# One gathered column of every two chunks (layer 0) and of every three (layer 1) is fetched by SyncE, row by row

## The reference

```python
zs = ZU[:, src, :]
zd = ZU[:, dst, :]
logits = (zs * zd).sum(-1) / scale
...
msgs = x[src]
summed = jax.ops.segment_sum(msgs, dst, num_segments=num_nodes)
```

## Time and profile before

| | us |
|---|---|
| median of the runs | 4623.81 |
| the profiled execution's own time | 4618.69 |
| its span | 4616.9 |
| POOL busy | 3353.7 (73%) |
| DVE busy | 2277.8 (49%) |
| PE busy | 930.4 (20%) |
| ACT busy | 778.7 (17%) |

### The profile page before, as it was taken

The page is one execution under the profiler, slowest core; times in us unless marked ns, Lnnn a source line. Parts: engine busy times, 40 slices in busy tenths (PEclk is TensorE's granted clock), DMA queues, the critical chain, the costliest instruction groups (busy, mean ns, idle before and its releaser), DMA issues. The chain is left out here.

```text
span 4616.9 us, 27468 instructions
## 1 busy us (share of the span) xinstructions
PE 930.4 (20%) x3111; PEld 610.2 (13%) x3111; DVE 2277.8 (49%) x9483; ACT 778.7 (17%) x1408; POOL 3353.7 (73%) x3541
## 2 busy tenths in 40 slices
PE   7301101112111000000094211222222221112037
PEld 7201001001001000000042100111111110001025
DVE  2107665665665565566563443443344344334447
ACT  2001001001001000000043222222222222222225
POOL 6677777777777777777565777777777777777765
PEclk6556555555556555555586555555555555555569
DMA  9713333333333222222275666666665666666579
GB/s 350 303 37 120 120 93 94 120 93 94 120 104 96 84 88 77 79 88 88 74 248 192 219 215 236 231 209 215 236 231 206 234 229 207 235 236 213 197 244 316
DMA packets 329803, 793.61 MB, mean 172 GB/s; under 512 B 78246, under 2 KB 216843, under 8 KB 300228
## 3 DMA queue, kind: packets, MB, share of 16 engines
q1 hardware_dynamic: 149906, 378.14, 23.0%
q0 software_dynamic: 139488, 279.69, 20.4%
q10 hardware_dynamic: 40274, 134.62, 7.4%
HBM read 420.40 MB, written 371.83 MB: 172 GB/s over the span
## 5 line engine op out<-in xcount | busy, mean ns | idle before, releaser
L473 POOL DMA_INDIRECT sb_big<-x,sb_idx x1564 | 1481.3, 947 | 513.0 <-issue 476.4
L473 POOL DMA_INDIRECT sb_big<-zu_rows,sb_idx x1564 | 1479.4, 946 | 490.4 <-issue 476.1
L1300 DVE SCALAR_TENSOR_TENSOR ps_V<-ps_V,sb_keepc,sb_big 128x256 f32<-128x256 f32 x1518 | 747.8, 493 | 132.5 <-ACT sb_big L901 79.3
L901 ACT COPY sb_big<-ps_V 128x1024 f32<-128x1024 f32 (+1 forms) x414 | 399.7, 966 | 1309.6 <-DVE ps_V L1300 1306.4
L654 PE MATMUL ps_T<-sb_ident,sb_xg 128*128 128x128 f32 x392 | 114.2, 389 | 2445.3 <-DMA sb_xg<-x 1232.4
L1300 DVE SCALAR_TENSOR_TENSOR ps_V<-ps_E,sb_keepc,sb_big 128x256 f32<-128x256 f32 x46 | 22.7, 492 | 1041.8 <-DMA sb_big<-x,sb_idx 1002.2
L1067 DVE TENSOR_TENSOR sb_big<-ps_V,sb_big 128x2176 f32<-128x2176 f32 x46 | 111.5, 2424 | 591.9 <-DMA sb_big<-zu_rows,sb_idx 591.9
L654 PEld LDWEIGHTS ps_T<-sb_ident,sb_xg 128*128 128x128 f32 x392 | 71.6, 200 | 2502.9 <-issue 1738.1
L1061 DVE TENSOR_TENSOR_SCAN ps_V<-ps_V,sb_big 128x34 f32<-128x34 f32 x2944 | 356.9, 208 | 17.4 <-issue 17.4
L1110 DVE TENSOR_TENSOR_SCAN sb_big<-ps_E,sb_big 128x34 f32<-128x34 f32 x2944 | 355.3, 203 | 1.6
L473 POOL DMA_INDIRECT sb_hn<-rows,sb_nidx x196 | 191.4, 976 | 87.6 <-issue 54.9
(11 more groups left out here) (229 smaller groups left out, 1732.5 us busy)
## 6 DMA issues: line engine op xcount, KB each, us to landing
rows<-sb_big SPq DMA_DIRECT2D x46, 3072.0 KB, 10.6
rows<-sb_big SPq DMA_DIRECT2D x46, 1280.0 KB, 10.5
rows<-sb_big ACTq DMA_DIRECT2D x46, 1224.0 KB, 5.4
z_at_start<-sb_big ACTq DMA_DIRECT2D x46, 1088.0 KB, 8.5
sb_big<-z_at_start SPq DMA_DIRECT2D x46, 1088.0 KB
sb_xg<-in_x_dram SPq DMA_DIRECT2D x42, 768.0 KB
own<-sb_hn SPq DMA_DIRECT2D x28, 896.0 KB, 11.5
sb_big<-own SPq DMA_DIRECT2D x28, 896.0 KB
```

Source lines behind the costliest of these rows:

```text
L473: pool.indirect_dma_start(to, None, table, bass.IndirectOffsetOnAxis(ap=index.bitcast(U32), axis=0), **more).then_inc(done, 16)
L901: act.copy(slot1[s][:, cols, :], V0[:, first_word:first_word + width].rearrange("p (c f) -> p c f", f=D)).then_inc(col_copied, 1)
L1300: dve.scalar_tensor_tensor(out=sums_at(j), in0=before, scalar=keepc[:, j:j + 1], in1=slot1[s][:, j, :], op0=ALU.mult, op1=ALU.add).then_in ...
```

## The change

After the change POOL gathers one column fewer in the second chunk of pairs 1 to 22 of layer 0, and one fewer in slot 1 of triples 0 to 14 of layer 1. SyncE fetches these columns in its place.

VectorE multiplies the row numbers of these columns by the length of a row once (`row_bytes`). For a column SyncE issues one transfer that lays its 128 byte offsets side by side in partition 0 (`stage_rows`), waits for it, then loads 16 offsets at a time into registers and issues one transfer per row, from the table at the offset in the register to one partition (`fetch_rows`).

In layer 0 the rows go to a tile of their own, `zx`; ScalarE copies it to the last column of `zs[1]` (`zx_copied`), VectorE waits for that copy before the product, and SyncE waits for it before it fetches the next. `fetch_zx(i)` brings the column of pair i+1 and stands behind `bg_load(0, i)` and ahead of `load_zd(i+1)`. In layer 1 the rows go straight to the last column of `slot1[1]`; `fetch_row1(i+1)` stands behind the stores of triple i and ahead of `bg_store(1, i)` and `bg_load(1, i+1)`, and waits until slot 1 of triple i is stored. VectorE waits for `row_fetched[1]` before slot 1's last column.

```diff
@@ -75,6 +75,8 @@
     GC = 4
     NGC = -(-C // GC)
     LOOK = S1 * C
+    RB = 16
+    U8 = mybir.dt.uint8
     NZ = 4
     assert FP * FQ == NF and FQ * FW <= C * F and CA % GC == 0 and NGC % 2 == 1 and C % GC == 2 and NG * GB == NB and NG % 2 == 0 and NCH % 2 == 0 and NG < NCH // S1 and 0 < ELAST <= COLS and NF * FW == E
     assert E <= EP and D == 2 * P
@@ -191,6 +193,9 @@
         end_i = sb("end_i", [P, 1], I32)
         keep_all = sb("keep_all", [P, 1])
         idx = [sb(f"idx{s}", [P, C], I32) for s in range(S1)]
+        row_bytes = [sb(f"row_bytes{k}", [P, n], I32) for k, n in ((0, NCH // 2), (1, NCH // S1))]
+        stage = sb("stage", [1, 2, P], I32)
+        zx = sb("zx", [P, F])
         nidx = [sb(f"nidx{s}", [P, GB], I32) for s in range(2)]
         zcar0 = sb("zcar0", [P, F])
         scar = sb("scar", [P, F + H])
@@ -275,6 +280,8 @@
         idx1_ready = sems("idx1_ready", S1); r_gathered = [sems(f"r_gathered{k}_", S1) for k in range(2)]
         keepc_made = sem("keepc_made"); col_summed = sem("col_summed"); col_copied = sem("col_copied")
         r_stored = sems("r_stored", S1); car1_saved = sem("car1_saved")
+        rows_scaled = sem("rows_scaled"); stage_loaded = sems("stage_loaded", 2); row_fetched = sems("row_fetched", 2)
+        zx_copied = sem("zx_copied")
         DA = 15
         NW = 5
 
@@ -283,6 +290,9 @@
         gate = sem("gate")
 
         block = ctx.enter_context(nc.Block())
+
+        def zs_landed(i, s):
+            return 16 * (C + (C - s) * i)
 
         def edge_cols(dram, c):
 
@@ -368,24 +378,55 @@
             sp.wait_ge(z_scattered, 16 * NB)
             sp.wait_ge(zcar_loaded, 16)
 
+            rows_at = [sp.alloc_register(f"row{k}") for k in range(RB)]
+
+            def stage_rows(layer, i):
+                with nc.allow_non_contiguous_dma(reason="a word of each partition"):
+                    sp.dma_start(stage[0:1, layer, :], row_bytes[layer][:, bass.ds(i, 1)]
+                                 ).then_inc(stage_loaded[layer], 16)
+
+            def fetch_rows(layer, to, table, width):
+                flat = table.rearrange("(a n) f -> a (n f)", a=1).bitcast(U8)
+                for p0 in range(0, P, RB):
+                    sp.load(rows_at, stage[0:1, layer, p0:p0 + RB])
+                    for k in range(RB):
+                        at_byte = sp.snap(rows_at[k], min_val=0, max_val=(N - 1) * 4 * width)
+                        sp.dma_start(to[p0 + k:p0 + k + 1, :].bitcast(U8), flat[:, bass.ds(at_byte, 4 * width)]
+                                     ).then_inc(row_fetched[layer], 16)
+
             def load_zd(i):
                 for s in range(2):
                     wait(sp, zd_used[s], i)
                     sp.dma_start(zd[s], edge_cols(z_at_start[0:EP, :], 2 * i + s)).then_inc(zd_loaded[s], 16)
 
+            def fetch_zx(i):
+                stage_rows(0, i + 1)
+                sp.wait_ge(stage_loaded[0], 16 * (i + 1))
+                sp.sem_inc(gate, 1)
+                wait(sp, zx_copied, i)
+                sp.sem_inc(gate, 1)
+                fetch_rows(0, zx[:, :], zu_rows, F)
+
             load_zd(0)
             bg_load(0, 0)
+            sp.wait_ge(rows_scaled, 2)
+            fetch_zx(0)
             with sp.Fori(1, NG - 1) as i:
                 load_zd(i)
                 bg_store(0, i - 1)
                 bg_load(0, i)
+                fetch_zx(i)
             load_zd(NG - 1)
             bg_store(0, NG - 2)
             bg_load(0, NG - 1, rows=TAIL)
+            fetch_zx(NG - 1)
             load_zd(NG)
             bg_store(0, NG - 1)
-            with sp.Fori(NG + 1, NCH // 2) as i:
+            fetch_zx(NG)
+            with sp.Fori(NG + 1, NCH // 2 - 1) as i:
                 load_zd(i)
+                fetch_zx(i)
+            load_zd(NCH // 2 - 1)
 
 
             def node_in(layer, i, s, rows=P):
@@ -415,6 +456,14 @@
                 sp.wait_ge(n_stored[0][s], 32 * (NG // 2))
 
 
+            def fetch_row1(i):
+                stage_rows(1, i)
+                sp.wait_ge(stage_loaded[1], 16 * (i + 1))
+                sp.sem_inc(gate, 1)
+                wait(sp, r_stored[1], 32 * i)
+                sp.sem_inc(gate, 1)
+                fetch_rows(1, slot1[1][:, C - 1, :], x1, D)
+
             def store_rows1(i, s):
                 c = S1 * i + s
 
@@ -425,14 +474,22 @@
                 sp.dma_start(edge_cols(rows1, c)[:, CA:C, :], slot1[s][:, CA:C, :]).then_inc(r_stored[s], 16)
 
             bg_load(1, 0)
+            fetch_row1(0)
             for s in range(S1):
                 store_rows1(0, s)
-            with sp.Fori(1, NG) as i:
+            fetch_row1(1)
+            with sp.Fori(1, NG - 1) as i:
                 bg_store(1, i - 1)
                 bg_load(1, i)
                 for s in range(S1):
                     store_rows1(i, s)
+                fetch_row1(i + 1)
+            bg_store(1, NG - 2)
+            bg_load(1, NG - 1)
+            for s in range(S1):
+                store_rows1(NG - 1, s)
             bg_store(1, NG - 1)
+            fetch_row1(NG)
             for k in range(S1 * NG, NCH):
                 store_rows1(k // S1, k % S1)
             sp.wait_ge(mend_dma, 64)
@@ -484,7 +541,8 @@
                 pool.wait_ge(idx_ready[s], i + 1)
                 wait(pool, sums_done[s], i)
                 pool.sem_inc(gate, 1)
-                for j in range(C):
+                first = isinstance(i, int) and i == 0
+                for j in range(C if s == 0 or first else C - 1):
                     gather(zs[s][:, j, :], zu_rows, idx[s][:, j:j + 1], zs_gathered[s])
 
             pool.wait_ge(zu_stored, 16 * NG)
@@ -537,7 +595,7 @@
                 pool.wait_ge(idx1_ready[s], i + 1)
                 wait(pool, r_stored[s], 32 * i)
                 pool.sem_inc(gate, 1)
-                for j in range(C):
+                for j in range(C - 1 if s == 1 else C):
                     gather(slot1[s][:, j, :], x1, idx[s][:, j:j + 1], r_gathered[int(j >= CA)][s])
 
             rounds(pool, NCH // S1, lambda i: [gather_rows1(i, s) for s in range(S1)])
@@ -797,7 +855,7 @@
                 for b in range(GB + 1):
                     background_step(layer, g, b)
 
-            def weights_of_edges(i, with_background):
+            def weights_of_edges(i, with_background, fetched=True):
                 for s in range(2):
 
                     act.wait_ge(diff_done, 2 * (2 * i + s + 1))
@@ -814,16 +872,20 @@
                     act.wait_ge(max_stored, 2 * i + s + 1)
                     act.dma_start(edge_cols(rows0, 2 * i + s), row0[s]).then_inc(rows0_stored[s], 16)
 
-                    act.wait_ge(zs_gathered[s], 16 * C * (i + 1))
+                    act.wait_ge(zs_gathered[s], zs_landed(i, s))
                     act.copy(idx[s][:, :], src_i[:, bass.ds((2 * i + s + 2) * C, C)]).then_inc(idx_ready[s], 1)
                     if with_background and s == 0:
                         background(0, i)
+                    if s == 1 and fetched:
+                        act.wait_ge(row_fetched[0], 16 * P * (i + 1))
+                        act.copy(zs[1][:, C - 1, :], zx[:, :]).then_inc(zx_copied, 1)
 
             weights_of_edges(0, True)
             with act.Fori(1, NG) as i:
                 weights_of_edges(i, True)
-            with act.Fori(NG, NCH // 2) as i:
+            with act.Fori(NG, NCH // 2 - 1) as i:
                 weights_of_edges(i, False)
+            weights_of_edges(NCH // 2 - 1, False, fetched=False)
 
 
             scale = 1.0 / float(R) ** 0.5
@@ -1037,6 +1099,10 @@
                                              ).then_inc(w_dve, 1)
 
 
+            for k, step, width in ((0, 2, F), (1, S1, D)):
+                last_cols = src_i[:, 0:NCH // step * step * C].rearrange("p (i c) -> p i c", c=step * C)[:, :, 2 * C - 1]
+                dve.tensor_scalar(row_bytes[k][:, :], last_cols, float(4 * width), None, ALU.mult
+                                  ).then_inc(rows_scaled, 1)
             dve.memset(scar[:, :], 0.0)
             done(dve.memset(mx[1][:, :, C:C + 1], LOWEST))
             dve.wait_ge(zcar_loaded, 16)
@@ -1063,7 +1129,9 @@
                     dve.wait_ge(zd_filled, c + 1)
                     dve.tensor_copy(zcar, zd_full[:, C - 1, :]).then_inc(zcar_saved, 1)
 
-                    dve.wait_ge(zs_gathered[s], 16 * C * (i + 1))
+                    dve.wait_ge(zs_gathered[s], zs_landed(i, s))
+                    if s == 1:
+                        wait(dve, zx_copied, i)
                     dve.tensor_tensor(zd[s], zd_full, zs[s], ALU.mult).then_inc(product_done, 1)
                     dve.wait_ge(product_done, c + 1)
                     dve.tensor_reduce(logit[:, :, :].rearrange("p h c -> p c h"),
@@ -1289,7 +1357,9 @@
                         dve.wait_ge(r_gathered[0][s], 16 * CA * (i + 1))
                         dve.wait_ge(car1_saved, c + 1)
                     elif j == CA:
```

(4 more changed lines are left out.)

## The result

The changed kernel takes 4839.65 us (median of four runs, 4835.98 to 4842.29) against 4624.55 us for the kernel before (four runs, 4594.52 to 4627.98). The ratio is 1.048 with an interval of 1.044 to 1.053: slower by 4.8%. Its profiled execution took 4842.29 us (span 4840.1) against 4618.69 before, 223.6 us more. Runs of one kernel lie further apart than the 0.3% named above: the kernel before took from 4592.09 to 4659.49 us in 17 runs on one chip. Part of that shows in the traces of all ten kernels: from the last gather of layer 0 to the first of layer 1, a stretch of node work that no edit is about, they took between 199 and 245 us (214.3 both before and after the change).

The account below looks back on a forecast made before the run. POOL's gathers, one every 1.25 us, were taken to bound both layers. From 4618.7 us, layer 0's -22 and layer 1's +355 gave 4952, about 4955 as a median; range 4660 to 5430.

Parts of the forecast that it names:

- Rival 1: Both layers: the fetch is wholly hidden, a row costs 0.29 us with registers free; 4572 us, chance 0.14.
- T: SyncE's time per fetched column, first register load to last row's issue: 69 us, between 37 and 99.
- Rival 2: Both layers: register loads are dear, 2.8 us each, 81 us per fetched column; total 5295 us, chance 0.20.
- Own store and background load to X: Layer 1, after the fetch: own store, background load and its landing, until ACT's first background block; 15 us, between 11 and 18.
- X: Layer 1: the moment ACT takes its first block of the background load; first one forecast 65 us late, at 3076.
- X to the last store's issue: Layer 1: from ACT's first background block through the sums of three slots, copy and store issue; 63 us.
- Staging: Layer 1: landing of the transfer laying a column's offsets in one partition, before the register loads; 7 us.
- Jump: SyncE's jump back over a long loop body, once per layer 1 cycle; 3 us.
- the 157 forecast: Layer 1: whole cycle from one fetch to the next, 157 us against POOL's 126.3, so 31 us too long.
- The other two terms: Layer 1: first background block 65 us late at the start; POOL catching up at the end, -59 us.
- Layer 0: Fetch covered at POOL's pace: -27.5 us for 22 gathers, +5 for the first pair, -22 in all.
- Each us of T moves it by 13: Layer 1: every microsecond of SyncE's fetch time per column changes the forecast loss by 13 us.

Follow-up runs that it names:

- The run with 160 rows: Changed kernel, with layer 0's first 32 rows of each column fetched once more to a tile of their own: 5097.69 us, ratio 1.102.
- with 96 rows: Changed kernel's order, but layer 1 fetches 96 rows per column to an unread tile and POOL gathers all columns: 4639.41 us, ratio 1.005.

## Why the prediction was right, and where it was too high

- **The mechanism and its place: right.** The forecast named fetch_row1(i+1) ahead of bg_load(1, i+1) and the chain from there through three sums. The profile shows TensorE, ScalarE and VectorE waiting in that order, POOL waiting for the store, and the exchange of the two calls takes the whole loss away.
- **POOL's share: right.** 46.3 us, 1.0%, was the price of 37 gathers and so the most that could be won. With the two calls exchanged the ratio is 0.989 (0.984 to 0.995); in its trace POOL's layer 0 is 29.9 us shorter than before (27.5 forecast) and its layer 1, at 1935.1, 21.7 us (18.8 forecast). The stretch between the layers took 23 us more in that execution, which was the slowest of the six. Rival 1, that all of this is hidden from the start, needed T under 38.
- **T: 62.5 us in layer 1 and some 64 in layer 0, not 69.** A row came every 0.40 us (0.238 the issue, two register copies of 0.03 and the steps between), not 0.46: the 0.21 us between two issues that I took from the earlier trace rows had a slower register instruction in it (0.055 us where the fetch has a copy of 0.034). The loads were 1.23 us each, 10 in all, as taken. Rival 2 (2.8 us each) is out. The Trainium skill's page "Runtime: NRT & Kernel Launch", section "Instruction fetch mechanics", has about 200 ns a register, which as an estimate is 3.2 us for sixteen. The trace does not agree, and the measurement decides: 1.23 us, 77 ns each, from SBUF.
- **Own store and background load to X: 9.9 us, not 15** (3089.39 to 3099.27). Behind a fetch the queue is empty, and the load's second issue takes 1.29 us where the earlier trace rows had 7.86. I had taken the middle of 11 and 18, both from rows with stores or loads just ahead.
- **X to the last store's issue: 62.1 us, forecast 63** (3099.27 to 3161.37). The sums ended at X + 19.9, X + 42.2 and X + 60.9; forecast 20, 42.5 and 61.5.
- **Staging: 11.7 us, not 7** (3012.21 to 3023.9). It stands behind 4 MB of stores and landed at 3023.6, the last of them at 3022.3, 10.6 us after its issue; at the first fetch of layer 1, with no store ahead, it landed in 5.1. The store's 10.5 us stood in the earlier trace rows, and I took less than that row says.
- **Jump: 3.1, forecast 3** (3086.3 to 3089.4).
- The sum: 62.5 + 9.9 + 62.1 + 11.7 + 3.1 = 149.3, against the 157 forecast. Layer 1 came out 100 us below its forecast (+255 for +355), and the cycle is most of that: by TensorE's first transposes, twelve cycles took 1792.8 us where 12 x 157 is 1884. The other two terms were near: the background's block of triple 1 came 63 us later after the layer's first gather than before the change (65 forecast), and from triple 13's to the last gather it took 68 us less (59). The step that was mis-sized is the cycle's 157, by T and the landing of the background load, with the staging's error partly making up for them.
- **Layer 0: -29.8, forecast -22.** 1507 gathers in 1881.7 us are one every 1.249 us: POOL waited for nothing, and the 5 us that I had put down for the first pair never came. SyncE's round was 82.5 us (rows of two pairs start at 678.60 and 761.12), forecast 83.3, against POOL's 83.8. That it came so near is partly luck: T was 63.9 and not 69, but from the first zd load to the staging it took 8.4 us and not 5.3, and from there to the first register load 7.1 and not 6. The late zd load was covered, as forecast (it landed in 6.4 us in the median, where I had 10), but not for nothing: VectorE now waits 214.3 us for it in all, and 403.3 instead of 591.9 for the gathers. It is idle time of about the same length under another name, and POOL did not see it. The margin is thin: 1.3 us in this pair, and next to none in others, whose rounds took up to 83.8. The run with 160 rows shows that what goes over it is paid. The rows of the page, the first of them of the kernel before, and of SyncE's queue beside the earlier trace rows:

```profile
L1067 DVE TENSOR_TENSOR sb_big<-ps_V,sb_big 128x2176 f32<-128x2176 f32 x46 | 111.5, 2424 | 591.9 <-DMA sb_big<-zu_rows,sb_idx 591.9
```

```profile
L1135 DVE TENSOR_TENSOR sb_big<-ps_V,sb_big 128x2176 f32<-128x2176 f32 x46 | 111.5, 2424 | 403.3 <-DMA sb_big<-zu_rows,sb_idx 403.3
...
L1119 DVE COPY ps_V<-sb_keep 128x34 f32 (+1 forms) x46 | 9.5, 206 | 242.4 <-DMA sb_big<-z_at_start 214.3
```

```profile
678.60 62.51 SPq L394 DMA_DIRECT2D sb_zx<-zu_rows  x128
744.23 2.26 SPq L400 DMA_DIRECT2D sb_big<-z_at_start  x2
...
747.99 4.51 SPq L340 DMA_DIRECT2D sb_xg<-in_x_dram  x1
752.64 0.56 SPq L385 DMA_DIRECT2D sb_stage<-sb_row_bytes  x1
761.12 19.62 SPq L394 DMA_DIRECT2D sb_zx<-zu_rows  x41
```

- "Each us of T moves it by 13": with T at 46.0 and 76.2 us the kernel took 4639 and 5040 us, 13.3 for each us of T. The changed kernel, with T at 62.5, lies between them at 4840 (in it VectorE waits for the rows and POOL gathers a column less). The break-even of T = 38 was not run; with 96 rows POOL still waited 57 us in all.

## What to carry to other kernels

An engine that only issues transfers has idle time in its waits, but its program is a queue: ask of each stretch of new work not how long it is but what stands behind it and who needs that. Work that nobody waits for soon goes behind the load that starts the next stage and not ahead of it; here two calls in the other order turned +4.8% into -1.1%. When two engines take turns, add up the whole cycle from one fetch to the next: while it is under the period of the engine that bounds the kernel the work is free, and each microsecond over it is paid in every round.

## What the runs showed of the hardware that I had not expected

A load of 16 registers from one partition of SBUF took SyncE 1.23 us in the median of 296. Some took longer: 4.0 to 4.8 us where the load stood right behind 4 MB of stores (the run with the staging ahead), and 3.2 us as the first load in the last six pairs of layer 0, with nothing of the kind in front. The runs do not say what makes a load slow. One-row transfers at an address in a register went out every 0.40 us with 1024 bytes (0.238 us the issue), and hardly faster with 256 (0.225). 128 such transfers in a row left no trace in the gathers of layer 1 beside them: 945 ns each, 947 before. A transfer of 128 words from SBUF to SBUF landed in 5.1 us with no store ahead of it in SyncE's queue, and in 11.1 to 11.5 behind the 4 MB of a slot's stores (thirteen of the other fourteen fetches).
